# A windowed attention stack on one core: the mask written by ScalarE, the norms read back in one transfer, a fourth front buffer, and a new order of all engines

## The chip, the core and the metric

The kernel runs on one core of one Trainium2 chip. The metric is the device time of the whole program in microseconds (us), lower is better; every run is one execution of the same program. The core has five engines that work side by side and wait for each other through semaphores: TensorE (PE in the rows, PEld for its weight loads), VectorE (DVE), ScalarE (ACT), GpSimd (POOL), and SyncE (SP), which here issues every DMA transfer. SPq in the rows is SP's queue issuing a transfer.

## What is computed

The program has two phases. The first is a dense causal attention layer with 16 heads over 4 batches of 512 tokens, width 128, with a residual. The change hardly touches it. The second is a stack of 6 layers, each of a local attention and a feed-forward block:

```python
q, k = l2norm(q) * qs, l2norm(k) * ksc          # norm over the 64 lanes of a head
q = q*cos*scale + rotate_half(q)*sin*scale      # k alike, with 1/scale
sim = einsum('bhwie,bhwje->bhwij', bq, bk2)*8   # 32 queries x 64 keys: own window and the one before
attn = softmax(where(mask, -big, sim))          # band mask
x = x + (attn @ v) @ Wo ; then layer norm, W1, a*gelu(gate), W2
```

Everything is float32, but for the mask, which is kept as bfloat16 zeros and -1e25.

## The kernel before

**Tiles and steps.** The second phase is cut into 24 steps (6 layers by 4 batches), each step into 4 tiles of 128 tokens: 96 tiles `g`. For each tile there is one front `f`: fronts come in pairs for half a sequence (256 tokens), an even `f` makes the keys, an odd `f` the queries. Tile pair `2hu`, `2hu+1` needs fronts `2hu` and `2hu+1`.

**A front.** `pe_front` multiplies by the weights into PSUM in four parts; ACT squares each part (`act_square`, L785), DVE multiplies it by the two rotary tables (`dve_products`, L799 and L800, into `T1` and `T2`), POOL adds the turned half (`pool_rotate`, L805). `pe_square_sums` (L813) adds the squares of each head. Then the inverse root is made: `dve_clamp`, `act_guess` (Ln, L826, and Exp, L828) and three DVE steps of `dve_newton`, the last at L837, into `RN`. The inverse norms go out to a small DRAM tensor `norms` (`sp_norms_out`, L843) and come back spread over all 128 partitions into `RB` (`sp_norms_in`, L850, four transfers of 32 partitions). `pool_scale` (L857) multiplies `T1` by `RB`. `sp_relayout` moves `T1` to the places of keys (`KZ`, 8 transfers, L876) or queries (`QP`, 4 transfers, L870). `RB` is one buffer: the load for `f` waits until `pool_scale(f-1)` is done.

**A tile.** `pe_scores` (L906 to L918) fills a PSUM bank for each half of the heads: four bf16 matmuls of `identb` by `band` (L912) write the mask, 16 matmuls add the scores. DVE takes the maximum and subtracts it, ACT takes the exponential, DVE sums, POOL normalises (L955), PE turns the probabilities (`pe_turn_probs`, L965), ACT keeps them, and `pe_values` (L990) multiplies by `U`, which `pe_u` (L891) makes in four parts, each kept by ACT (L898).

**The feed-forward block** of each step is spread over later tiles: turn (L1083), six up products one after another through PSUM bank 6 (L1109), gelu on ACT (L1115, which loads its table), gate on DVE, down (L1131). `next_vo` (L1010) makes the weights of a later step.

**The order** is written out by hand: `pe_slot(k)`, `act_slot(k)`, `dve_slot(k)`, `pool_slot(k)` and `sp_slot(k)` list what each engine does for slot `k`, one slot per tile. An engine takes its list strictly in order, so a wait holds everything behind it. The lines that set the order of SP:

```python
def sp_slot(k):
    if hold_f(k + 4): sp_norms_in(k + 4)
    ...
    if hold_f(k + 5): sp_norms_out(k + 5)
    if hold_f(k + 4): sp_relayout(k + 4)
```

Of the kernel before, what the change touches and what calls it, by code (L numbers as in the profile page):

```python
# [52 lines left out]
def build(nc, x, wq, wk, wv, wr, w1, w2, b2, rot, qsc, wqk, wvt, wos, lngt, lnbt, b1t, out):  # L53
    pe, act, dve, pool, sp = nc.tensor, nc.scalar, nc.vector, nc.gpsimd, nc.sync
    with ExitStack() as keep:
# [4 lines left out]
        XM = sb('XM', [P, TILES, E])  # L60
# [74 lines left out]
        with ExitStack() as ctx:  # L135
# [233 lines left out]
            def act_early_keep(b):  # L369
                r = slice(b * TPB, (b + 1) * TPB)  # L370
                act.wait_ge(s_res, PAIRS * (b + 1))
                act.activation(XM[:, r, :], X[:, r, :], ACT.Copy).then_inc(s_exm, 1)

            def act_dense_program():
                act_ln_keep(0)
                for h in range(-3, 2 * UNITS + 3):
# [19 lines left out]
                    if side == 0 and PAIRS <= u < UNITS and u % PAIRS == 4:  # L396
                        act_early_keep(u // PAIRS - 1)
# [68 lines left out]
            def dve_early_scale(b, t):  # L466
                dve.wait_ge(s_erstd, b + 1)
                dve.wait_ge(s_exm, b + 1)
# [128 lines left out]

            def sp_dense_program():
# [8 lines left out]
                for q in range(HG):  # L607
                    sp.wait_ge(s_vod, q)
                    in_dma(sp, s_vo0, WVS[:, :], wvt[q])
                    in_dma(sp, s_vo0, WOS[:, :], wos[q])  # L610

# [17 lines left out]
        with ExitStack() as ctx:  # L629
# [5 lines left out]
            T1 = [sbl(f'T1{i}', [P, HG, 2, HALF]) for i in range(3)]  # L635
# [21 lines left out]
            norms = [nc.dram_tensor(f'norms{i}', (P, HALF), F32).ap() for i in range(2)]  # L657
# [28 lines left out]
            l_scores_done = sig('scl', 2, 'pe', 5)  # L686
            l_max_done = sig('nml', 2, 'dve')
# [29 lines left out]
            lxm = sig('lxm', 1, 'act')  # L717
# [69 lines left out]
            def dve_products(f, i):  # L787
# [3 lines left out]
                if i == 0:  # L791
                    dve.wait_ge(l_folded.sem, l_folded.at(s // BATCH * 4 + 2 * hf + kind))
                    if f >= 3 and kind:
                        dve.wait_ge(s_kz, 128 * ((f - 3) // 2 + 1))
                    elif f >= 3:
                        dve.wait_ge(s_qp, 64 * ((f - 3) // 2 + 1))
                dve.wait_ge(l_squared.sem, l_squared.at(f, i))
                dve.wait_ge(l_rotated.sem, l_rotated.at(f, i - 2))
                dve.tensor_tensor(T1[f % 3][:, i, :, :], v, TAB[:, kind, 0, :, cols], ALU.mult)  # L799
                dve.tensor_tensor(T2[i % 2][:, :, :], v, TAB[:, kind, 1, :, cols], ALU.mult).then_inc(l_products.sem, 1)  # L800

            def pool_rotate(f, i):
                pool.wait_ge(l_products.sem, l_products.at(f, i))
                t1 = T1[f % 3][:, i, :, :]
# [34 lines left out]
            def sp_norms_out(f):  # L839
                sp.wait_ge(l_newton.sem, l_newton.at(f))  # L840
                if f >= 2:
                    sp.wait_ge(s_rb, 64 * (f - 1))
# [406 lines left out]
            def act_slot(k):  # L1249
                if here(k):  # L1250
                    act_exp(*tile(k), 1)
# [305 lines left out]
```

## Time and profile before

| what | value |
|---|---|
| median of 3 runs | 2100.08 us (2099.58 to 2102.47) |
| the profiled execution: own time / span of the core | 2099.16 us / 2097.3 us |
| granted TensorE clock, mean | 0.989 |
| busy share of PE, DVE, ACT, POOL | 97%, 72%, 63%, 69% |
| first phase, filling, steady tiles, tail | to about 511, to 560, to about 2072, to 2097.3 us |

The profiled execution took 1.9 us more than its span, outside the span. Matmuls are pipelined and their ends are modelled, so PE's busy share says less than the distance from the start of one group of matmuls to the start of the next.

### The profile page before, as it was taken

What the parts mean: (1) busy time and instruction counts of PE and PEld (TensorE: products, weight loads), DVE (VectorE), ACT (ScalarE), POOL (GpSimd) and SP (SyncE); (2) the same over time, 40 slices, a digit from 0 to 9 for tenths busy, and PEclk for the clock granted to TensorE, in tenths of its full rate; (3) what the DMA queues carried; (4) which work ended last, traced back from release to release, by engine and by line L of the source; (5) the groups of instructions that cost most, each with busy time, mean ns of one, the idle gap of its engine ahead of it and who ended that gap; (6) DMA issues with size and microseconds to landing.
All of it is one profiled execution on the core that took longest, in us unless ns stands there. A gap on an engine that the chain in (4) does not pass through costs nothing.

```text
span 2097.3 us, 61286 instructions
## 1 busy us (share of the span) xinstructions
PE 2029.8 (97%) x23760; PEld 1292.7 (62%) x23760; DVE 1501.0 (72%) x3291; ACT 1330.2 (63%) x2522; POOL 1453.3 (69%) x1439
## 2 busy tenths in 40 slices
PE   8999999998689999999999999999999999999997
PEld 4555555554456666666666666666666666666654
DVE  5666666665677777777877777877777877777853
ACT  5666666665356567666667676667666667666654
POOL 3344443433678888878877888878977888878852
PEclk9999999999799999999999999999999999999999
DMA  4000000000444554455454464454644455444441
GB/s 134 6 1 6 1 1 6 1 1 6 109 108 123 144 151 110 123 129 159 124 127 110 127 175 117 119 126 126 172 120 107 122 139 160 121 121 118 120 109 28
DMA packets 218416, 204.96 MB, mean 98 GB/s; under 512 B 32403, under 2 KB 211601, under 8 KB 218129
## 3 DMA queue, kind: packets, MB, share of 16 engines
q1 hardware_dynamic: 218128, 201.04, 37.1%
q8 instruction: 191, 3.13, 0.6%
q14 instruction: 97, 0.79, 0.1%
HBM read 83.53 MB, written 13.63 MB: 46 GB/s over the span
## 4 chain that ended last, share of the span: by engine, by line
SPq 25%; POOL 20%; DMA 14%; PE 12%; issue 3%; ACT 0%; DVE 0%; DVEq 0%; ACTq 0%; POOLq 0%
POOL T L857 20%; DMA RB<-norms 14%; SPq L876 10%; SPq L850 8%; SPq L870 7%; PE bank L891 3%; PE bank L779 3%; PE bank L1109 1%; PE bank L918 1%; PE bank L990 1%; PE bank L965 1%; PE bank L1131 1%; PE bank L813 1%; PE bank L912 0%; PE bank L1010 0%
## 5 line engine op out<-in xcount | busy, mean ns | idle before, releaser
L857 POOL TENSOR_TENSOR T<-T,RB 128x512 f32<-128x512 f32 x384 | 480.4, 1285 | 213.8 <-DMA RB<-norms 213.8
L805 POOL TENSOR_TENSOR T<-T 128x512 f32<-128x512 f32 x384 | 491.7, 1283 | 78.4 <-DVE T L800 78.0
L891 PE MATMUL bank<-WU,XT 128*32 128x512 f32 x3072 | 414.3, 599 | 2.0 <-ACT U L898 1.9
L779 PE MATMUL bank<-XT,WQK 128*128 128x256 f32 x1536 | 401.0, 394 | 14.7 <-DVE T L800 13.1
L539 POOL TENSOR_SCALAR PR<-PR,RI 128x512 f32<-128x512 f32 x256 | 174.1, 694 | 291.0 <-DVE RI L439 289.9
L785 ACT ACTIVATE SQ<-bank 128x512 f32<-128x512 f32 x384 | 224.9, 600 | 237.4 <-PE bank L779 236.9
L779 PEld LDWEIGHTS bank<-XT,WQK 128*128 128x128 f32 x1536 | 277.2, 192 | 136.3 <-issue 68.5
L799 DVE TENSOR_TENSOR T<-bank,TAB 128x512 f32<-128x512 f32 x384 | 261.8, 682 | 124.5 <-ACT SQ L785 67.6
L898 ACT ACTIVATE U<-bank 128x512 f32<-128x512 f32 x384 | 228.8, 596 | 96.4 <-PE bank L891 95.8
L363 ACT ACTIVATE PR<-PR,NM 128x512 f32<-128x512 f32 x256 | 183.5, 718 | 147.1 <-DVE NM L434 145.7
L800 DVE TENSOR_TENSOR T<-bank,TAB 128x512 f32<-128x512 f32 x384 | 261.2, 680 | 0.0
L434 DVE CUSTOM_DVE_ANT_0 PR<-bank,causal 128x512 f32<-128x512 f32 x256 | 170.3, 684 | 108.8 <-PE bank L247 108.8
L918 PEld LDWEIGHTS bank<-KZ,QP 128*32 128x32 f32 x6144 | 177.2, 111 | 67.6 <-issue 51.4
L955 POOL TENSOR_TENSOR PL<-PL,RIL 128x512 f32<-128x512 f32 x192 | 202.4, 1055 | 20.2 <-DVE RIL L948 19.9
L990 PEld LDWEIGHTS bank<-U,PTL 128*32 128x32 f32 x5952 | 171.7, 110 | 58.4 <-issue 58.4
L918 PE MATMUL bank<-KZ,QP 128*32 128x128 f32 x6144 | 204.5, 274 | 0.0
L925 DVE TENSOR_REDUCE NML<-bank 128x8 f32<-128x512 f32 x192 | 131.9, 687 | 99.5 <-PE bank L918 99.4
L990 PE MATMUL bank<-U,PTL 128*32 128x128 f32 x5952 | 185.3, 273 | 0.8 <-issue 0.8
L972 ACT ACTIVATE PTL<-bank 128x512 f32<-128x512 f32 x192 | 114.2, 595 | 65.4 <-PE bank L965 65.2
L254 PEld LDWEIGHTS bank<-ident,PR 128*128 128x128 f32 x1024 | 112.8, 141 | 65.6 <-POOL PR L539 40.3
L1109 PE MATMUL bank<-XNT,W1S 128*114 128x512 f32 (+1 forms) x288 | 151.0, 609 | 2.3 <-ACT GE L1115 1.0
L945 DVE TENSOR_REDUCE RSL<-PL 128x8 f32<-128x512 f32 x192 | 130.4, 679 | 15.6 <-ACT PL L939 15.6
(124 smaller groups left out, 3059.0 us busy)
## 6 DMA issues: line engine op xcount, KB each, us to landing
RB<-norms SPq DMA_DIRECT2D x384, 128.0 KB, 3.3
KZ<-T SPq DMA_DIRECT2D x384, 128.0 KB, 2.5
QP<-T SPq DMA_DIRECT2D x192, 256.0 KB, 4.7
TAB<-rotary_dram SPq DMA_DIRECT2D x24, 512.0 KB, 5.2
norms<-RN SPq DMA_DIRECT2D x96, 128.0 KB, 1.7
WQK<-wqk_halves_dram SPq DMA_DIRECT2D x12, 512.0 KB, 6.2
WVS<-wv_turned_dram SPq DMA_DIRECT2D x29, 128.0 KB, 3.4
WOS<-wo_lanes_dram SPq DMA_DIRECT2D x29, 128.0 KB, 3.5
```

The lines of the kernel that those rows point to most:

```text
L779: m = pe.matmul(b[:, ab * HALF:(ab + 1) * HALF], WQK[n % 3][:, i, ab, :], XT[s % 2][:, hf * HALF:(hf + 1) * HALF], start=True, stop=True)
L785: act.activation(SQ[i][:, :, :], bank[5 * (i % 2)][:, :].rearrange('p (a c) -> p a c', a=2), ACT.Square).then_inc(l_squared.sem, 1)
L799: dve.tensor_tensor(T1[f % 3][:, i, :, :], v, TAB[:, kind, 0, :, cols], ALU.mult)
L800: dve.tensor_tensor(T2[i % 2][:, :, :], v, TAB[:, kind, 1, :, cols], ALU.mult).then_inc(l_products.sem, 1)
L805: pool.tensor_tensor(t1, t1, T2[i % 2][:, ::-1, :], ALU.add).then_inc(l_rotated.sem, 1)
L857: pool.tensor_tensor(t1, t1, RB[:, i:i + 1, :].to_broadcast([P, 2, HALF]), ALU.mult).then_inc(l_scaled.sem, 1)
L876: sp.dma_start(kz[:, :, pp, :], T1[f % 3][r:r + WIN, :, ab, :]).then_inc(s_kz, 16)
L891: i = pe.matmul(bank[1][h * WIN:(h + 1) * WIN, :], XT[s % 2][:, c0:c0 + WIN], WU[:, lp * HG + h, :], start=True, stop=True)
L898: act.activation(U6[(4 * g + w) % 6][:, :], bank[1][:, :], ACT.Copy).then_inc(l_u_kept.sem, 1)
L918: m = pe.matmul(o[:, 2 * pl:2 * pl + 2, :, :], QP[t // 2][:, pr, q0:q0 + WIN], KZ[t // 2][:, pr, :, q0:q0 + GRP].rearrange('p h (k j) -> p ...
L955: pool.tensor_tensor(o, o, r, ALU.mult).then_inc(l_probs_normed.sem, 1)
L990: i = pe.matmul(bank[7][w * WIN:(w + 1) * WIN, 0:E], PTL[half][:, 2 * k + gg, w * WIN:(w + 1) * WIN], u[:, grp * E:(grp + 1) * E], start=f ...
```

## The change

1. **Mask.** `act_mask(s, t, half)` lets ACT copy `band` (bf16) into the PSUM bank; `pe_scores` waits for it and its four mask matmuls are gone. All later matmuls add to the bank.
2. **Norms.** `norms` is now 32 rows of 4 x 256 values, so that the four rows in use are each one piece of 4 KB; they come back in one transfer that reads each row 32 times.
3. **Buffers.** `T1` has four buffers instead of three. Room comes from `XM`, the copy of the residual, which moves to a DRAM tensor `resid`: SP stores it (three times in the first phase, once between the phases) and loads it at the end into the first `T1` buffer. Four copies by ACT go.
4. **Order.** All five slot functions are written anew; the loops begin at slot -7 instead of -8.

The diff, cut to its core:

```diff
-            T1 = [sbl(f'T1{i}', [P, HG, 2, HALF]) for i in range(3)]
+            T1 = [sbl(f'T1{i}', [P, HG, 2, HALF]) for i in range(4)]
...
-            norms = [nc.dram_tensor(f'norms{i}', (P, HALF), F32).ap() for i in range(2)]
+            norms = [nc.dram_tensor(f'norms{i}', (WIN, HG * HALF), F32).ap() for i in range(2)]
...
-                sp.dma_start(norms[f % 2], RN[:, :]).then_inc(s_rn, 16)
+                sp.dma_start(norms[f % 2].rearrange('h (g c) -> g h c', g=HG), RN[:, :]).then_inc(s_rn, 16)
...
-                rows = norms[f % 2].rearrange('(g h) (a c) -> h a g c', h=WIN, a=1)
-                for h in range(HG):
-                    sp.dma_start(RB[h * WIN:(h + 1) * WIN, :, :], rows[h].to_broadcast([WIN, HG, HALF])).then_inc(s_rb, 16)
+                rows = norms[f % 2][0:HG, :].rearrange('h (a q) -> h a q', a=1).to_broadcast([HG, WIN, HG * HALF])
+                sp.dma_start(RB[:, :, :].rearrange('p g c -> p (g c)'), rows).then_inc(s_rb, 16)
...
+            def act_mask(s, t, half):
+                g = s * TPB + t
+                act.wait_ge(l_shifted.sem, l_shifted.at(g - 1, half))
+                act.activation(bank[2 + half][:, :], band[:, 0 if t == 0 else 1, :], ACT.Copy).then_inc(l_masked.sem, 1)
+
...
-                pe.wait_ge(l_shifted.sem, l_shifted.at(g - 1, half))
-                for w in range(4):
-                    r = slice(w * WIN, (w + 1) * WIN)
-                    pe.matmul(sbk[r, :], identb[:, r], band[:, 0 if t == 0 else 1, :], start=True, stop=False, skip_group_check=True)
+                pe.wait_ge(l_masked.sem, l_masked.at(g, half))
```

What the new slots do to the order is seen in the built programs. First **PE**, from the scores of one tile on (`WU,XT` is a part of `U`, `KZ,QP` the scores, `SQ,IND` the sums of squares, `XT,WQK` parts of a front, `U,PTL` the values, `ident,PL` the turned probabilities). Before:

```order
L891 MATMUL bank<-WU,XT 32x512 x4
L912 MATMUL bank<-band,identb 32x512 x4
L918 MATMUL bank<-KZ,QP 32x2x2x32 x16
L813 MATMUL bank<-SQ,IND 32x256 x8
L891 MATMUL bank<-WU,XT 32x512 x4
L912 MATMUL bank<-band,identb 32x512 x4
L918 MATMUL bank<-KZ,QP 32x2x2x32 x16
L779 MATMUL bank<-XT,WQK 128x256 x4
L891 MATMUL bank<-WU,XT 32x512 x4
L990 MATMUL bank<-U,PTL 32x128 x32
L891 MATMUL bank<-WU,XT 32x512 x4
L779 MATMUL bank<-XT,WQK 128x256 x2
```

And now, from the last sums of squares of a tile on:

```order
L817 MATMUL bank<-SQ,IND 32x256 x8
L894 MATMUL bank<-WU,XT 32x512 x4
L923 MATMUL bank<-KZ,QP 32x2x2x32 x32
L894 MATMUL bank<-WU,XT 32x512 x4
L995 MATMUL bank<-U,PTL 32x128 x14
L783 MATMUL bank<-XT,WQK 128x256 x4
L1136 MATMUL bank<-W2S,GE 128x128 x6
L995 MATMUL bank<-U,PTL 32x128 x14
L894 MATMUL bank<-WU,XT 32x512 x4
L970 MATMUL bank<-ident,PL 128x128 x4
L783 MATMUL bank<-XT,WQK 128x256 x2
L1136 MATMUL bank<-W2S,GE 128x128 x6
```

The masks are gone, both halves of the scores stand together at the head of the tile, the probabilities of the same tile are turned later in the same slot, and the sums of squares of the front stand at its end.

Then **SP**, in the middle of a layer change (`norms<-RN` goes out, `RB<-norms` comes back, `KZ<-T` and `QP<-T` are the relayouts, `TAB` and `WQK` are tables and weights). Before:

```order
L843 DMA norms<-RN 128x256
L870 DMA QP<-T 64x4x256 x4
L850 DMA RB<-norms 32x4x256 x4
L113 DMA TAB<-rotary_dram 128x4x256
L843 DMA norms<-RN 128x256
L876 DMA KZ<-T 32x4x256 x8
L850 DMA RB<-norms 32x4x256 x4
```

And now:

```order
L847 DMA norms<-RN 4x32x256
L113 DMA TAB<-rotary_dram 128x4x256
L853 DMA RB<-norms 128x1x1024
L879 DMA KZ<-T 32x4x256 x8
L847 DMA norms<-RN 4x32x256
L113 DMA TAB<-rotary_dram 128x4x256
L853 DMA RB<-norms 128x1x1024
L873 DMA QP<-T 64x4x256 x4
```

The load of `RB` stood behind the relayout of the front before; now it stands ahead of it, directly behind the norms that it waits for, and is one transfer instead of four.

Last **ACT**, around the slot in which gelu and the guess meet (`ACT_TABLE_LOAD` loads a function table; `LG<-SM` is the Ln and `bank<-LG` the Exp of the guess). Before:

```order
L898 ACTIVATE U<-bank 128x512
L1115 ACTIVATE GE<-bank,B1T 114x512
L826 ACT_TABLE_LOAD
L826 ACTIVATE LG<-SM 128x256
L828 ACT_TABLE_LOAD
L828 ACTIVATE bank<-LG 128x256
L898 ACTIVATE U<-bank 128x512
L939 ACTIVATE PL<-PL 128x512
L785 ACTIVATE SQ<-bank 128x512 x2
L898 ACTIVATE U<-bank 128x512
L939 ACTIVATE PL<-PL 128x512
L1115 ACT_TABLE_LOAD
L1115 ACTIVATE GE<-bank,B1T 113x512
```

And now:

```order
L1120 ACTIVATE GE<-bank,B1T 114x512
L901 ACTIVATE U<-bank 128x512
L830 ACT_TABLE_LOAD
L830 ACTIVATE LG<-SM 128x256
L832 ACT_TABLE_LOAD
L832 ACTIVATE bank<-LG 128x256
L901 ACTIVATE U<-bank 128x512
L1120 ACT_TABLE_LOAD
L1120 ACTIVATE GE<-bank,B1T 113x512
L1122 ACT_TABLE_LOAD
L901 ACTIVATE U<-bank 128x512
L944 ACTIVATE PL<-PL 128x512
```

The two table loads of the guess were followed by a part of `U`, the exponential and squares, and only then by the third gelu; now the third gelu with two more loads comes directly behind that part of `U`, ahead of the next exponential. `bank<-band` is the new mask copy.

## Rows read from the trace of the kernel before

**Rows 1.** The page: busy time, and the chain that ended last
```profile
PE 2029.8 (97%) x23760; PEld 1292.7 (62%) x23760; DVE 1501.0 (72%) x3291; ACT 1330.2 (63%) x2522; POOL 1453.3 (69%) x1439
...
SPq 25%; POOL 20%; DMA 14%; PE 12%; issue 3%; ACT 0%; DVE 0%; DVEq 0%; ACTq 0%; POOLq 0%
```

**Rows 2.** Windows: each engine in the steady stretch, (x) instructions
```profile
700.00:1900.00 1200.00, 1194.13 (x16652) 802.57 (x16648) 926.31 (x1864) 798.73 (x1407) 992.12 (x896) 1.00 0.51 132
```

**Rows 3.** Windows: L918 alone, the same stretch (PE, PEld)
```profile
700.00:1900.00 1200.00, 160.68 (x4864) 139.21 (x4864) 1.00 0.51 132
```

**Rows 4.** Timeline of PE over most of a tile (start, length, what)
```profile
1112.45 1.02 PE L1109 MATMUL bank<-XNT,W1S 128*114 128x512 f32 x2
1113.31 1.03 PE L779 MATMUL bank<-XT,WQK 128*128 128x256 f32 x4
...
1114.70 1.06 PE L891 MATMUL bank<-WU,XT 128*32 128x512 f32 x8
1115.58 0.40 PE L912 MATMUL bank<-band,identb 128*32 128x512 bf16 x4
1115.80 1.06 PE L918 MATMUL bank<-KZ,QP 128*32 128x128 f32 x32
1116.67 1.05 PE L813 MATMUL bank<-SQ,IND 128*32 128x256 f32 x16
1117.54 1.04 PE L891 MATMUL bank<-WU,XT 128*32 128x512 f32 x8
1118.39 0.40 PE L912 MATMUL bank<-band,identb 128*32 128x512 bf16 x4
1118.61 1.06 PE L918 MATMUL bank<-KZ,QP 128*32 128x128 f32 x32
1119.60 1.99 PE L779 MATMUL bank<-XT,WQK 128*128 128x256 f32 x8
```

**Rows 5.** Chain of waits, 1100 to 1135 (start, length, what)
```profile
by line: POOL T L857 35.8%; DMA RB<-norms 28.5%; SPq L876 16.4%; SPq L850 11.9%; SPq L870 10.2%; issue 3.2%; SPq L847 0.1%
...
1101.46 5.02 POOL T L857 x4
...
1114.24 3.54 DMA RB<-norms
...
1117.85 4.99 POOL T L857 x4
...
1129.52 3.19 DMA RB<-norms
...
1132.78 2.53 POOL T L857 x2
```

**Rows 6.** Timeline of SP's issues in the same stretch
```profile
1106.50 6.07 SPq L876 DMA_DIRECT2D KZ<-T  x8
1112.67 2.01 SPq L850 DMA_DIRECT2D RB<-norms  x4
...
1122.85 3.71 SPq L870 DMA_DIRECT2D QP<-T  x4
1126.66 3.30 SPq L850 DMA_DIRECT2D RB<-norms  x4
```

**Rows 7.** The page: DMA issues (count, size of one, us to landing)
```profile
RB<-norms SPq DMA_DIRECT2D x384, 128.0 KB, 3.3
KZ<-T SPq DMA_DIRECT2D x384, 128.0 KB, 2.5
QP<-T SPq DMA_DIRECT2D x192, 256.0 KB, 4.7
...
norms<-RN SPq DMA_DIRECT2D x96, 128.0 KB, 1.7
```

**Rows 8.** Timeline of ACT where gelu and guess meet
```profile
1117.06 1.28 ACT L826 ACT_TABLE_LOAD   x1
1118.35 0.42 ACT L826 ACTIVATE LG<-SM 128x256 f32<-128x256 f32 x1
1118.79 1.28 ACT L828 ACT_TABLE_LOAD   x1
1120.08 0.39 ACT L828 ACTIVATE bank<-LG 128x256 f32<-128x256 f32 x1
1120.41 0.58 ACT L898 ACTIVATE U<-bank 128x512 f32<-128x512 f32 x1
```

**Rows 9.** Timeline of DVE: last step of that Newton, and of the next
```profile
1121.42 0.42 DVE L837 SCALAR_TENSOR_TENSOR RN<-Y,bank 128x256 f32<-128x256 f32 x1
...
1136.05 0.42 DVE L837 SCALAR_TENSOR_TENSOR RN<-Y,bank 128x256 f32<-128x256 f32 x1
```

**Rows 10.** Timeline of SP in the filling of the pipeline
```profile
536.77 5.99 SPq L876 DMA_DIRECT2D KZ<-T  x8
542.87 1.97 SPq L850 DMA_DIRECT2D RB<-norms  x4
```

**Rows 11.** Windows: a QP relayout, and a stretch with one narrow transfer
```profile
556.00:557.00 1.00, 1.00 (x4) 0.82 (x3) 1.00 (x4) 0.00 (x0) 1.00 (x2) 0.50 0.88 180
658.90:660.20 1.30, 1.30 (x8) 1.07 (x7) 1.27 (x3) 0.97 (x2) 1.30 (x2) 1.00 0.08 23
```

**Rows 12.** Groups of the page: busy, mean ns of one, idle before and releaser
```profile
L857 POOL TENSOR_TENSOR T<-T,RB 128x512 f32<-128x512 f32 x384 | 480.4, 1285 | 213.8 <-DMA RB<-norms 213.8
L805 POOL TENSOR_TENSOR T<-T 128x512 f32<-128x512 f32 x384 | 491.7, 1283 | 78.4 <-DVE T L800 78.0
...
L898 ACT ACTIVATE U<-bank 128x512 f32<-128x512 f32 x384 | 228.8, 596 | 96.4 <-PE bank L891 95.8
...
L955 POOL TENSOR_TENSOR PL<-PL,RIL 128x512 f32<-128x512 f32 x192 | 202.4, 1055 | 20.2 <-DVE RIL L948 19.9
...
L925 DVE TENSOR_REDUCE NML<-bank 128x8 f32<-128x512 f32 x192 | 131.9, 687 | 99.5 <-PE bank L918 99.4
```

**Rows 13.** Timeline of PE: next weights (L1010) and values (L990)
```profile
1103.15 1.16 PE L1010 MATMUL bank<-WOS,WVS 64*128 64x128 f32 x8
1104.24 2.00 PE L779 MATMUL bank<-XT,WQK 128*128 128x256 f32 x8
...
1123.26 1.93 PE L990 MATMUL bank<-U,PTL 128*32 128x128 f32 x64
1125.01 1.04 PE L891 MATMUL bank<-WU,XT 128*32 128x512 f32 x8
```

More of the change, by code:

```diff
@@ L1241, in pe_slot @@
                     pe_u(*tile(k - 1), 1)
+                    pe_turn_probs(*tile(k - 1), 0)
+                if step_at(k - 8, LAST - 1):
+                    pe_ffn_up((k - 8) // 4, 4)
+                if hold_f(k + 3):
+                    pe_front(k + 3, 2)
                 if step_at(k - 7, LAST - 1):
@@ L1259, in act_slot @@
                 if here(k):
-                    act_keep_probs(*tile(k), 0)
-                    act_keep_u(*tile(k), 1)
+                    act_keep_probs(*tile(k), 1)
                 if hold_f(k + 4):
                     act_square(k + 4, 3)
-                if here(k):
-                    act_keep_probs(*tile(k), 1)
-                if step_at(k + 2, LAST):
-                    act_boundary((k + 2) // 4)
+                if step_at(k - 6, LAST - 1):
+                    act_ffn_gelu((k - 6) // 4, 1)
@@ L1268, in act_slot @@
                 if here(k):
                     act_keep_u(*tile(k), 2)
-                if step_at(k - 6, LAST - 1):
-                    act_ffn_gelu((k - 6) // 4, 1)
-                if step_at(k - 5, LAST - 1):
-                    act_ffn_scale((k - 5) // 4)
+                if step_at(k - 1, LAST):
+                    act_boundary((k - 1) // 4)
+                if hold_f(k + 4):
+                    act_guess(k + 4)
+                if here(k):
+                    act_keep_u(*tile(k), 3)
@@ L1316, in dve_slot @@
+            def dve_slot(k):
                 if step_at(k - 9, LAST - 1):
                     dve_ffn_gate((k - 9) // 4, 1)
-                if here(k - 1):
-                    dve_max(*tile(k - 1), 0)
                 if step_at(k - 11, LAST - 2):
@@ L1322, in dve_slot @@
                 if hold_f(k + 2):
+                    dve_products(k + 2, 2)
                     dve_clamp(k + 2)
+                    dve_products(k + 2, 3)
+                    dve_newton(k + 2)
+                if here(k - 1):
+                    dve_max(*tile(k - 1), 0)
                 if half_at(k + 3):
@@ L1398, in pe_layers_program @@
             def pe_layers_program():
-                for k in range(-8, TOTAL + 3):
+                for k in range(-7, TOTAL + 3):
                     pe_slot(k)
@@ L1409, in act_layers_program @@
                 act.preload_act_table_set('natural_log_exp_and_others')
-                r = slice((BATCH - 1) * TPB, BATCH * TPB)
-                act.activation(XM[:, r, :], X[:, r, :], ACT.Copy).then_inc(lxm.sem, 1)
-                for k in range(-8, TOTAL + 3):
+                for k in range(-7, TOTAL + 3):
                     if k == 0:
@@ L1422, in dve_layers_program @@
             def dve_layers_program():
-                for k in range(-8, TOTAL + 4):
+                for k in range(-7, TOTAL + 4):
                     if k == 0:
@@ L1437, in pool_layers_program @@
                 pool.sem_inc(l_folded.sem, 4)
-                for k in range(-8, TOTAL + 3):
+                for k in range(-7, TOTAL + 3):
                     pool_slot(k)
@@ L1444, in sp_layers_program @@
             def sp_layers_program():
+                r = slice((BATCH - 1) * TPB, BATCH * TPB)
+                sp.dma_start(resid[:, r, :], X[:, r, :]).then_inc(s_xm, 16)
                 sp_next_vo(0)
-                for k in range(-8, TOTAL + 3):
+                for k in range(-7, TOTAL + 3):
                     sp_slot(k)
+                sp_resid_back()
                 sp_shift(LAST)
```

235 lines of the change are left out of this document (118 added, 117 removed).

## The prediction

> **What bounds the kernel now.** I read the page first. PE is busy 97% of the span, the others 63 to 72%, yet the chain that ended last runs mostly over SP's queue, POOL and DMA and only 12% over PE [rows 1]. Two things can thus be the bound, and each has to be measured in the steady stretch, 700 to 1900 us.
>
> A tile takes 64 score matmuls of L918; 4864 of them in 1200 us are 76 tiles, so a tile takes 15.79 us [rows 3], and the 96 tiles about 1515 us. POOL works 992.12 us there, 13.05 per tile, DVE 12.2, ACT 10.5 [rows 2]: none is full.
>
> PE: busy shares of modelled ends prove little, so I take distances between starts in the timeline [rows 4]. A part of U takes 0.88 or 0.85 us, a half of the scores 0.87 and 0.99, the sums of squares 0.87, two parts of a front 1.83 or less. Four lanes of 32 columns run side by side in the first three; a 512-column f32 product on full width (L1109) takes 0.86. So a column costs the same wherever I look, and nothing stands between the groups: PE is at its column rate, with only tenths of a microsecond lost where a group changes. It is a true bound, or within some tenths of a microsecond of one.
>
> The other candidate is a ring through SP. In the chain of waits, 1101 to 1133, every piece begins where the one before ends: POOL scales front f (5.0 us), SP issues the relayout of f (6.07 us for keys, 3.71 for queries), then the four loads of RB (2.01 or 3.30), the last lands 3.2 to 3.5 after its issue, POOL scales f+1 [rows 5, 6]. From 1101.46 to 1132.78 are two fronts, 15.66 us each. POOL's wait for RB before each front, 213.8 us in all, 2.2 per front, is this ring [rows 12]. So before, PE and the ring are both at their limit, and a gain needs both to give way.
>
> **What the change does, part by part.**
>
> *Masks.* The four mask matmuls take 0.22 and 0.22 us from start to start (1115.58 to 1115.80, 1118.39 to 1118.61) [rows 4]: 0.44 per tile, 96 tiles, 42 us off PE. ACT takes two copies of 128x512 more. No row copies from SBUF into a bank at that size: the nearest are L898 (596 ns, from a bank) and the Exp of the guess, which writes 256 columns of a bank in 0.39 us [rows 8, 12], so 0.6 each, at the most 0.78. ACT goes from 10.5 to 11.7 us per tile. This lies beside PE, since the copy for the next tile stands between the exponentials, a slot ahead. If that cover went, each copy would hold up the scores by its 0.6.
>
> *SP's ring.* RB for f+1 is now asked for ahead of the relayout of f, so the ring is scale, one issue (0.5), landing, scale. Even with a landing of 8 us it is 5.0+0.5+8 = 13.5: it no longer binds. Three issues of about 0.5 go from SP too. What binds in its place is a longer path: the relayout of f now stands behind norms out and RB in of f+1, hence behind the Newton steps of f+1. The path is: sums of squares of f+1, Newton, norms out, RB issue, relayout of f, scores. The order gives it one whole tile and a piece: from the end of the sums in one slot, over the next slot, past U (0.88) and an up product (0.86) or the next weights (1.1), and an up product behind the sums in the worst tile: some 18 us [rows 4, 13]. The terms: Newton ends 4.3 us after the sums in the tile where gelu takes the table away (1117.54 to 1121.84), else 2.9 (1133.55 to 1136.47), and one more tenth or three since a product stands in between [rows 4, 9]; norms out 1.7 [rows 7]; RB's issue 0.5; relayout of queries to the last landing 2.3 + 4.7 = 7.0, and 2 more because RB's 512 KB are ahead of it. That is 15.7 in the worst tile: 2 us to spare. Of the fourth buffer: products of f need the relayout of f-4 landed, not f-3; since the relayout is later by some 5 us now, this pays for the delay, and costs nothing itself.
>
> *The single transfer.* It is the unknown cost. Before, four transfers take 1.4 us of issue and 3.3 of landing, 4.7 to 5 together [rows 6, 7]. Lower bound: the 1.7 of norms out, for a quarter of the bytes. Upper bound: all goes over few engines. One row shows what a narrow transfer does: with 0.08 of 16 engines busy, one and a little more, 23 GB/s flow [rows 11]. Four engines would need 131 KB each at 22, 6.0 us; the ends are what norms out takes beside its 8 KB per engine, 1.7 - 0.4 = 1.3; together 7.3. I take 5 to 6 as its effect on POOL: RB is needed about 6 us after it is asked for, since four rotations of 1.28 and two normalisations of 1.05 (7.2 us) now stand between two scales [rows 12].
>
> *Order.* The turned probabilities are now due in the same slot as their scores. Between scores and turning PE has U, half the values, two front parts, half the values and U again: 0.87+0.9+1.8+0.9+0.88, 5.4 us and the second half's scores, 0.87: 6.2 us or more [rows 4, 13]. The chain beside it is maximum, shift, exponential, sum, reciprocal on DVE and ACT, each 0.6 to 0.7 (six of them), then POOL's 1.05: 4.7 to 5.5 us [rows 12]. It fits. The one place where it doesn't is the slot after the gelus. ACT makes the guess with two table loads (1117.06 to 1120.47) [rows 8], then keeps the last part of U and at once loads again, the third gelu, and loads again: 3.4 us of work ahead of the next exponential. PE waits there for U, for the up product that needs the bank, or for the probabilities; laid side by side I get 0.5 us, once per four tiles, 24 x 0.5 = 12 us.
>
> *Residual in DRAM.* Four copies of 0.6 go off ACT, which has room; the transfers are 256 KB, issued a batch before they are needed; the one between the phases is hidden by the fill, 50 us long. Nothing.
>
> *Fill.* The first load of RB after a relayout of keys starts 6 us after it could (536.77 to 542.87) [rows 10]; that comes forward. The relayout of queries on which the first scores wait goes back behind the next norms, by about as much. Nothing, plus or minus 5.
>
> **Sum.** 2099.2 - 42 + 12 = 2069 of its own time; the median of the runs shown lies 0.9 above the profiled one: 2070. As a tile: 15.79 - 0.44 + 0.13 = 15.48.
>
> **The rivals.**
>
> *The wide transfer turned narrow (slower), 0.28.* If RB comes over four engines, the relayout behind it queues on those four. They have 6.0 us of RB and then 64 KB of relayout each. A relayout of queries flows at 180 GB/s with 0.88 of the engines busy [rows 11], 11 to 13 GB/s for each: 5.3 us more, so that the last piece lands 0.8+6.0+5.3+0.5 = 12.6 us after RB's issue. Norms out, in four blocks now, would take 1.1 more. Then the path is 4.4+2.8+0.1+12.6 = 19.9 in the worst tile and 18.7 in the other that waits, against 18: 1.9 and 0.7 too late, 2.6 per four tiles, 0.65 per tile, 62 us, and 5 for the fill: 2137. If those four engines go at 22 GB/s once alone, the path just fits. It decides against the change from a mean delay of 0.3 us per tile on. For it speaks that RB's source has four rows as its outer step; against it, that the path has slack if the engine rate is the higher one. The Trainium skill (DMA: Bandwidth & Descriptors, "Why a DMA increments its semaphore by 16 and not by 1") says that the number of engines is the largest up to 16 that divides the slowest dimension of both sides: here 4. By that rule the narrow case is the one that happens, and only its price is open; the trace's narrow stretch agrees with it, but no run here shows it for RB. The same page, "Rules for kernel authors", advises one 128-partition transfer in place of several to part of the partitions, by which the single one would be no slower.
>
> *All waits vanish, 0.15.* The small losses at group changes that I read as PE's own are partly the ring's, and the guess costs nothing: 15.2 us per tile, -57 us, 2043; with half of it 2050.
>
> *Nothing gained, 0.10.* Another chain holds the old pace, most likely DVE to ACT to POOL for the probabilities, since they lost a slot of slack: 0.44 per tile eaten, 2097 to 2101.
>
> **How the numbers follow.** Likeliest, 0.47: PE bound, masks gone, small waits: 2070, its own range 2058 to 2088. The measurement tells about 0.2%, 4 us, from no change. Faster is the likeliest and the vanishing waits, 0.62; same is most of the third, 0.08; slower is the narrow case and the rest, 0.30. The range reaches down to 2050, which leaves out 0.05, and up to 2125, where the narrow case is half through, which leaves out some 0.13.
>
> **What the profile after would show.** PE: distances as before, no L912, a tile of 15.3 to 15.5 us. POOL's wait for RB below 0.5 us per front. SP's ring no longer in the chain, PE in its place. RB landing at 5 to 6 us; at 7 or more the narrow case is on, and the scores (L923) would wait for QP's landing, which they never do now. ACT between the third gelu and the next exponential: if PE stands there more than 1 us, the third term was too small. I am wrong altogether if a tile takes 15.8 us or more with PE waiting in one place of every slot.

## The result, and the profile after

The changed kernel takes 2360.66 us (median of 4 runs, 2353.85 to 2365.46) beside 2101.27 for the one before (4 runs, 2099.58 to 2103.76): ratio 1.1224, 95% interval [1.1196, 1.1253]. It is slower by 259 us, where 2070 was forecast and the range ended at 2125.

The page, busy time and chain, which answers to [rows 1]:

```profile
PE 2098.2 (89%) x22992; PEld 1315.0 (56%) x22992; DVE 1503.6 (64%) x3291; ACT 1433.8 (61%) x2708; POOL 1454.6 (62%) x1439
...
PE 54%; DMA 10%; issue 8%; POOL 4%; DVE 1%; SPq 1%; ACT 1%; DVEq 0%; ACTq 0%; POOLq 0%
```

SP's queue has left the chain, as forecast, and PE is in its place. But PE now stands idle, 8% of the chain is "issue", and PE's busy time went up by 68 us although 768 matmuls are gone. Windows over the steady stretch, all engines first, then L923 (the scores, L918 before) alone; they answer to [rows 2, 3], and the two last numbers but one are the granted clock and the DMA share:

```profile
700.00:1900.00 1200.00, 1064.19 (x13558) 698.44 (x13559) 785.93 (x1578) 750.08 (x1321) 837.66 (x755) 0.93 0.49 110
...
700.00:1900.00 1200.00, 170.37 (x4096) 153.09 (x4096) 0.93 0.49 110
```

4096 score matmuls are 64 tiles: 18.75 us a tile, against 15.79. The groups of the page, and its DMA issues, answer to [rows 12, 7]:

```profile
L860 POOL TENSOR_TENSOR T<-T,RB 128x512 f32<-128x512 f32 x384 | 479.6, 1279 | 400.5 <-DMA RB<-norms 400.5
...
L923 PE MATMUL bank<-KZ,QP 128*32 128x128 f32 x6144 | 253.1, 333 | 192.4 <-issue 192.4
...
RB<-norms SPq DMA_DIRECT2D x96, 512.0 KB
KZ<-T SPq DMA_DIRECT2D x384, 128.0 KB, 4.8
QP<-T SPq DMA_DIRECT2D x192, 256.0 KB, 6.8
```

POOL's wait for RB rose from 213.8 to 400.5 us, 4.2 per front. The relayouts land after 4.8 and 6.8 us instead of 2.5 and 4.7. And PE waits 192.4 us ahead of the scores, in 48 places, up to 8.3 us each. Before, it waited 0.0 us at the scores and 10.7 us, in 14 places, at the mask matmuls that stood ahead of them. The waits stand in every second tile, as `pe_scores` waits for the landing of `KZ` and `QP` only in the first tile of a pair. The name "issue" hides the releaser; SP, POOL and PE together show it. SP:

```profile
1221.48 0.58 SPq L847 DMA_DIRECT2D norms<-RN  x1
1224.79 0.57 SPq L853 DMA_DIRECT2D RB<-norms  x1
1225.44 3.73 SPq L873 DMA_DIRECT2D QP<-T  x4
1235.80 0.57 SPq L847 DMA_DIRECT2D norms<-RN  x1
1242.39 0.56 SPq L853 DMA_DIRECT2D RB<-norms  x1
```

POOL, then PE, the same stretch (in brackets the idle time before, and its releaser):

```profile
1228.36 2.50 POOL L809 TENSOR_TENSOR T<-T 128x512 f32<-128x512 f32 x2 [0.21 <-DVE T L804]
1237.38 4.93 POOL L860 TENSOR_TENSOR T<-T,RB 128x512 f32<-128x512 f32 x4 [6.52 <-DMA RB<-norms]
```

```profile
1215.81 1.05 PE L817 MATMUL bank<-SQ,IND 128*32 128x256 f32 x16
...
1218.71 1.93 PE L923 MATMUL bank<-KZ,QP 128*32 128x128 f32 x64
...
1234.63 0.38 PE L752 MATMUL bank<-ident,X 128*128 128x128 f32 x2
1240.78 3.64 PE L923 MATMUL bank<-KZ,QP 128*32 128x128 f32 x64 [5.76 <-issue]
```

RB is issued at 1224.79 and POOL can start only at 1237.38, 12.6 us later. The queries behind it are all issued by 1229.17, yet the scores that need them start at 1240.78. The DMA view of 1224 to 1242, in 40 slices of 0.45 us (tenths of the 16 DMA engines busy, and GB/s), says why:

```profile
DMA  2000207889899999999993122222222222221100
GB/s 84 0 0 0 18 9 196 203 212 228 191 168 178 180 155 168 105 100 127 198 137 50 36 73 91 80 82 75 82 80 82 87 84 86 86 66 48 43 20 0
```

Near 1233.5 the busy share falls from 0.9 to between 0.1 and 0.3, and from 1234.4 to 1239.8 some 80 GB/s flow. The window below has the share as 0.25, which is four engines of 16, near 20 GB/s each: they work off what is left. From 1239.8 on the traffic thins, and the scores start at 1240.78. What still flows then, up to 1241.5, is most likely the norms going out, issued at 1235.80, on which RB's load waits until 1242.39.

The wait costs twice. Windows around the same scores, the numbers after POOL's being the granted clock, DMA share and GB/s:

```profile
1236.00:1240.70 4.70, 0.00 (x0) 0.00 (x0) 0.00 (x0) 0.00 (x0) 3.32 (x3) 0.74 0.25 77
1240.80:1244.30 3.50, 3.50 (x68) 3.50 (x72) 1.53 (x3) 0.00 (x0) 3.50 (x4) 0.50 0.06 16
1245.30:1250.00 4.70, 4.70 (x84) 3.26 (x76) 3.52 (x7) 3.73 (x7) 2.08 (x2) 1.00 0.84 184
```

PE was idle, the granted clock fell, and the scores ran at 0.50, the 1.2 GHz level: 3.64 us for the 64 matmul records that take 1.93 in the tile without the wait (1218.71). At 1245.3 the clock is 1.00 again.

### The profile page after: what moved, and what is told of

Same layout as the page of the kernel before. It is cut to its first block, busy times and chain, and to the rows that moved or that the text cites. A ratio compares the mean times of both kernels' runs of the same rounds, so it can differ in the third digit from the quotient of the medians.

```text
span 2363.3 us, 59655 instructions
## 1 busy us (share of the span) xinstructions
PE 2098.2 (89%) x22992; PEld 1315.0 (56%) x22992; DVE 1503.6 (64%) x3291; ACT 1433.8 (61%) x2708; POOL 1454.6 (62%) x1439
## 4 chain that ended last, share of the span: by engine, by line
PE 54%; DMA 10%; issue 8%; POOL 4%; DVE 1%; SPq 1%; ACT 1%; DVEq 0%; ACTq 0%; POOLq 0%
PE bank L894 12%; PE bank L783 12%; PE bank L923 8%; DMA RB<-norms 6%; PE bank L995 6%; PE bank L1114 5%; PE bank L970 4%; POOL T L860 3%; PE bank L817 3%; PE bank L1136 2%; DMA norms<-RN 2%; DMA WQK<-wqk_halves_dram 1%; PE bank L1015 1%; POOL T L809 1%; SPq L879 1%
## 5 line engine op out<-in xcount | busy, mean ns | idle before, releaser
L860 POOL TENSOR_TENSOR T<-T,RB 128x512 f32<-128x512 f32 x384 | 479.6, 1279 | 400.5 <-DMA RB<-norms 400.5
L809 POOL TENSOR_TENSOR T<-T 128x512 f32<-128x512 f32 x384 | 481.7, 1276 | 35.7 <-DVE T L804 35.7
L894 PE MATMUL bank<-WU,XT 128*32 128x512 f32 x3072 | 437.5, 628 | 4.4 <-ACT U L901 2.2
L923 PE MATMUL bank<-KZ,QP 128*32 128x128 f32 x6144 | 253.1, 333 | 192.4 <-issue 192.4
L783 PE MATMUL bank<-XT,WQK 128*128 128x256 f32 x1536 | 391.4, 388 | 30.8 <-DVE T L804 22.0
L923 PEld LDWEIGHTS bank<-KZ,QP 128*32 128x32 f32 x6144 | 227.7, 135 | 230.8 <-issue 230.8
L995 PE MATMUL bank<-U,PTL 128*32 128x128 f32 x5952 | 208.3, 276 | 0.0
L970 PEld LDWEIGHTS bank<-ident,PL 128*128 128x128 f32 x768 | 85.3, 141 | 111.9 <-POOL PL L960 86.9
```

The lines of the kernel that those rows point to most:

```text
L783: m = pe.matmul(b[:, ab * HALF:(ab + 1) * HALF], WQK[n % 3][:, i, ab, :], XT[s % 2][:, hf * HALF:(hf + 1) * HALF], start=True, stop=True)
L809: pool.tensor_tensor(t1, t1, T2[i % 2][:, ::-1, :], ALU.add).then_inc(l_rotated.sem, 1)
L860: pool.tensor_tensor(t1, t1, RB[:, i:i + 1, :].to_broadcast([P, 2, HALF]), ALU.mult).then_inc(l_scaled.sem, 1)
L894: i = pe.matmul(bank[1][h * WIN:(h + 1) * WIN, :], XT[s % 2][:, c0:c0 + WIN], WU[:, lp * HG + h, :], start=True, stop=True)
L923: m = pe.matmul(o[:, 2 * pl:2 * pl + 2, :, :], QP[t // 2][:, pr, q0:q0 + WIN], KZ[t // 2][:, pr, :, q0:q0 + GRP].rearrange('p h (k j) -> p ...
L995: i = pe.matmul(bank[7][w * WIN:(w + 1) * WIN, 0:E], PTL[half][:, 2 * k + gg, w * WIN:(w + 1) * WIN], u[:, grp * E:(grp + 1) * E], start=f ...
```

## The experiments

Each ratio is against the kernel before, run on the same chip. The medians come from different chips, on which the kernel before took 2101.27 to 2105.34 us; a difference between two experiments on different chips is therefore uncertain by some 4 us.

**Norms wide both ways** (`a_wide_both`, called the wide version below). The changed kernel with the old layout of `norms`, so that `RB` comes in four transfers; masks, buffers and order stay.

```diff
-            norms = [nc.dram_tensor(f'norms{i}', (WIN, HG * HALF), F32).ap() for i in range(2)]
+            norms = [nc.dram_tensor(f'norms{i}', (P, HALF), F32).ap() for i in range(2)]
-                sp.dma_start(norms[f % 2].rearrange('h (g c) -> g h c', g=HG), RN[:, :]).then_inc(s_rn, 16)
+                sp.dma_start(norms[f % 2], RN[:, :]).then_inc(s_rn, 16)
-                rows = norms[f % 2][0:HG, :].rearrange('h (a q) -> h a q', a=1).to_broadcast([HG, WIN, HG * HALF])
-                sp.dma_start(RB[:, :, :].rearrange('p g c -> p (g c)'), rows).then_inc(s_rb, 16)
+                rows = norms[f % 2].rearrange('(g h) (a c) -> h a g c', h=WIN, a=1)
+                for h in range(HG):
+                    sp.dma_start(RB[h * WIN:(h + 1) * WIN, :, :], rows[h].to_broadcast([WIN, HG, HALF])).then_inc(s_rb, 16)
```

> The changed kernel with the old way of the norms alone: out in one transfer of 128 rows, back in four transfers of 32 partitions each; mask, fourth buffer and new order stay. Theory N (the transfers with four blocks as their outer step run over few engines, and hold up what is queued behind them): norms out lands in 1.7 us, the last of RB about 5 us after its first issue, PE's wait ahead of the scores goes, and the time is what was predicted for the change without this, about 2070, at most 2085. Theory O (the new order is at fault: relayout behind the next norms, probabilities due in the same tile): no more than 40 us come back from 2361, since the waits stay.

2066.86 us (2065.58 to 2067.35), ratio 0.9817 [0.9803, 0.9832]. Its page, busy time, chain, groups and issues:

```profile
PE 2009.1 (97%) x22992; PEld 1242.9 (60%) x22992; DVE 1495.7 (72%) x3291; ACT 1430.7 (69%) x2708; POOL 1457.1 (71%) x1439
...
PE 71%; issue 1%; DVE 1%; POOL 1%; ACT 0%; DMA 0%; SPq 0%; DVEq 0%; POOLq 0%; ACTq 0%
...
L861 POOL TENSOR_TENSOR T<-T,RB 128x512 f32<-128x512 f32 x384 | 481.8, 1288 | 19.9 <-DMA RB<-norms 19.7
...
L924 PE MATMUL bank<-KZ,QP 128*32 128x128 f32 x6144 | 186.4, 273 | 0.4 <-issue 0.4
...
RB<-norms SPq DMA_DIRECT2D x384, 128.0 KB, 3.2
KZ<-T SPq DMA_DIRECT2D x384, 128.0 KB, 2.9
QP<-T SPq DMA_DIRECT2D x192, 256.0 KB, 4.8
```

So the shape of two transfers costs 294 us, more than the whole loss of 259, and the rest of the change is a gain. Of the 299.8 us between the two spans (2363.3 and 2063.5), 192.0 are PE's idle time ahead of the scores and 89.1 its longer busy time; the other 18.7 are idle times elsewhere. The busy time grew by 66.7 us in the scores and by 23.2 in `U` behind them (L894, 437.5 us there, 414.3 here), and hardly in the rest.

**One transfer with 32 outer rows** (`b_one_wide`). As above, but `RB` in a single transfer whose outer step is the 32 repeats, not the four rows. It reads other rows of `norms` than the kernel should.

```diff
+                flat = norms[f % 2].rearrange('(h g) c -> h (g c)', g=HG)[0:HG, :]
+                rows = flat.rearrange('(a h) q -> a h q', a=1).to_broadcast([WIN, HG, HG * HALF])
+                sp.dma_start(RB[:, :, :].rearrange('p g c -> p (g c)'), rows).then_inc(s_rb, 16)
```

> One transfer for RB, as in the change, with pieces of 4 KB, but the repeating dimension (32) outermost in place of the four rows; norms out as one transfer of 128 rows. RB so gets rows in another order than the lanes need, and the norms lie in DRAM otherwise: the numbers computed are other ones, the work is the same. Theory N in its form 'the outer dimension of four is what hurts': as fast as the kernel with four transfers, 2060 to 2085. Rival 'one big transfer of 512 KB is slow as such': RB lands 10 us or more after its issue, and the time stays above 2250.

2066.95 us (2065.36 to 2070.41), 0.9821 [0.9805, 0.9837]; RB lands 5.0 us after its issue, and the relayouts behind it after 3.9 and 5.9 us, 1.0 and 1.1 later than in the wide version, without a cost in time. Being one transfer costs nothing and wins nothing; with the same bytes and the same four rows, the order of the two outer steps makes the difference.

**The two halves of the shape** (`c_in_narrow`, `d_out_narrow`). First only `RB` comes in narrow (four outer rows, 32 repeats inside; it too reads other rows), while the norms go out wide; then the other way round, out as in the changed kernel, in by four transfers.

```diff
+                rows = flat.rearrange('h (a q) -> h a q', a=1).to_broadcast([HG, WIN, HG * HALF])
```

> The changed kernel with norms out in one transfer of 128 rows again, and RB back as in the change, four rows outermost, each read 32 times (the rows are others than the lanes need; the work is the same). It parts the two narrow transfers. Theory N with RB as its main part: RB takes 11 to 12.5 us as in the changed kernel, and the time is 2280 to 2340. If the norms going out were the main part (5.4 to 6.5 us in many fronts, where 1.7 had been): below 2200.

```diff
+                for h in range(HG):
+                    row = norms[f % 2][h:h + 1, :].to_broadcast([WIN, HG * HALF])
+                    sp.dma_start(RB[h * WIN:(h + 1) * WIN, :, :].rearrange('p g c -> p (g c)'), row).then_inc(s_rb, 16)
```

> The changed kernel with norms out as in the change (four blocks outermost), and RB back in four transfers of 32 partitions with pieces of 4 KB. Theory N with RB as its main part: norms out takes about 3 us, since no narrow RB lies ahead of it, and the path of the relayout has room for 1 us more: 2065 to 2100. If norms out is slow by itself (5 us or more in each front): 2150 or more.

In narrow: 2271.57 us (2262.7 to 2279.29), 1.079 [1.0754, 1.0825]. Out narrow: 2072.4 (2069.29 to 2073.38), 0.9846 [0.983, 0.9863]. The load makes 205 of the 294 us, a little less than expected (2280 to 2340 had been forecast for it). The store alone makes 5.5, but 89 once the load is narrow too. The likely reason, which no run isolates, is that its 128 KB then queue on engines that still have RB and the relayout: from 1235.80 to 1242.39 above, norms out take 6.6 us; before they took 1.7 [rows 7].

**Eight outer rows** (`h_eight`). The load reads eight rows 16 times each (other rows again).

```diff
+                rows = flat.rearrange('h (a q) -> h a q', a=1).to_broadcast([8, 16, HG * HALF])
```

> One transfer for RB as in the change, but with eight rows outermost, each read 16 times (other rows than the lanes need: the numbers are other ones, the bytes and pieces are the same); norms out as one transfer of 128 rows. Theory N (the outer dimension sets over how many engines it goes): with four rows RB took 11 to 12.5 us, with 32 repeats outermost 5.0; with eight it lands after 6.5 to 7.5, and the time is 2067 to 2110. Rival (the distinct rows outermost, with a repeat inside, are slow as such): above 2200 as with four.

2152.97 us (2151.38 to 2164.93), 1.025 [1.0225, 1.0275]. That is between the cases of 32 and 4 outer rows, above what was expected. How many engines each load keeps busy can be read in the filling of the pipeline, where RB is alone in flight. The windows, in order, are of the kernels with 32, 8 and 4 outer rows, and the three last numbers are granted clock, DMA share and GB/s:

```profile
528.50:530.50 2.00, 1.31 (x19) 0.52 (x17) 1.26 (x2) 0.60 (x1) 0.70 (x1) 1.00 0.86 256
531.00:534.00 3.00, 1.44 (x18) 0.62 (x18) 1.94 (x5) 1.29 (x4) 0.00 (x0) 1.00 0.52 138
531.00:535.00 4.00, 1.59 (x19) 0.62 (x18) 2.90 (x7) 1.78 (x4) 0.35 (x1) 1.00 0.25 98
```

Shares of 0.86, 0.52 and 0.25 are some 14, 8 and 4 engines of 16. So the outer rows do set the number of engines. But eight engines move 17 GB/s each and four move 25, so that twice the engines carry only 1.4 times as much; this is part of why eight rows come out so near to four.

**RB alone** (`i_rb_alone`). The narrow load, with SP waiting until it has landed before it issues the relayout. This tells whether RB's 11 to 12.6 us are its own or come of company.

```diff
                 sp.wait_ge(l_scaled.sem, l_scaled.at(f))
+                sp.wait_ge(s_rb, 16 * min(f + 2, FRONTS))
```

> As c_in_narrow (only RB's load is narrow, its rows others than the lanes need), but SP waits until RB of the next front has landed before it issues the relayout behind it, so that RB has the DMA engines for itself. Theory S (what is issued behind RB shares its few engines and makes it late): RB lands 7.5 to 9 us after its issue, as the first load of the filling does (7.8), where c_in_narrow had 11 to 12.6; the time is no better than 2230, since the relayout now begins later. Theory Q (four engines reading four rows are as slow as 11 us by themselves once all else runs): RB still takes 10.5 or more.

2354.32 us (2346.33 to 2360.58), 1.1184 [1.1161, 1.1207]. SP's timeline, where each relayout is issued when RB has landed:

```profile
1201.81 0.59 SPq L854 DMA_DIRECT2D RB<-norms  x1
1209.60 5.24 SPq L881 DMA_DIRECT2D KZ<-T  x8
...
1222.66 0.60 SPq L854 DMA_DIRECT2D RB<-norms  x1
1230.67 3.77 SPq L875 DMA_DIRECT2D QP<-T  x4
```

RB alone takes 7.8 and 8.0 us, and between 1014 and 1461, 24 of 25 loads take 7.4 to 8.6. In the kernel where only the load is narrow, eight loads issued between 1087 and 1214 took 10.8 to 12.9, so some 3 to 5 us come from transfers issued behind it. Here POOL's wait for RB falls to 78.3 us and relayouts land in 2.6 and 4.3; but they are issued 8 us later, and the scores wait all the same, 171.8 us. The path has no room for RB's time in either order.

**Narrow transfers in the kernel before** (`g_before_narrow`). Its order keeps the relayout ahead of RB, with no relayout behind.

```diff
-                rows = norms[f % 2].rearrange('(g h) (a c) -> h a g c', h=WIN, a=1)
-                for h in range(HG):
-                    sp.dma_start(RB[h * WIN:(h + 1) * WIN, :, :], rows[h].to_broadcast([WIN, HG, HALF])).then_inc(s_rb, 16)
+                rows = norms[f % 2][0:HG, :].rearrange('h (a q) -> h a q', a=1).to_broadcast([HG, WIN, HG * HALF])
+                sp.dma_start(RB[:, :, :].rearrange('p g c -> p (g c)'), rows).then_inc(s_rb, 16)
```

> The kernel before with its own order, mask and three buffers, and only the norms' transfers of the change: out in four blocks, back in one transfer with four rows outermost. Theory N: RB lands 10 us or more after its issue here too, and since the relayout (4.9 us of issue on the mean) stands inside the ring, a tile takes 5.0 + 4.9 + 0.6 + 10 to 12, 20.5 to 22.5 us, 2550 to 2750 in all: worse than in the new order. Rival (the transfer hurts only because the new order puts the relayout behind it): 2100 to 2200.

2439.92 us (2435.7 to 2448.56), 1.1608 [1.1582, 1.1633]. The chain of waits:

```profile
1206.87 4.99 POOL T L856 x4
...
1215.70 9.70 DMA RB<-norms
...
1225.47 5.05 POOL T L856 x4
...
1235.86 10.09 DMA RB<-norms
```

This is the ring of [rows 5] with 9.7 and 10.1 us for RB, issue and landing together, where it had 5.2 and 6.5 (issue 2.01 and 3.30, landing 3.2 to 3.5): 18.6 us for the front shown, which has the short relayout, and 19.2 on the mean (4004 score matmuls in the 1200 us from 700 on). The expectation of 2550 to 2750 us was too high, since it took 0.6 and 10 to 12 for issue and landing. That the transfer hurts only with a relayout behind it is refuted; the new order even takes the narrow transfers 79 us better than the old one does.

**The masks, and the ring** (`e_mask_pe`, `f_before_mask`). On the wide version, masks back on PE; and, on the kernel before, masks by ACT and nothing else.

```diff
-                pe.wait_ge(l_masked.sem, l_masked.at(g, half))
+                pe.wait_ge(l_shifted.sem, l_shifted.at(g - 1, half))
+                for w in range(4):
+                    r = slice(w * WIN, (w + 1) * WIN)
+                    pe.matmul(sbk[r, :], identb[:, r], band[:, 0 if t == 0 else 1, :], start=True, stop=False, skip_group_check=True)
```

> The changed kernel with the old way of the norms (as in a_wide_both), and the mask written by PE again, four bf16 matmuls per half ahead of the scores; the copies on ACT go. Theory M (PE's column time is the bound once the ring through SP is gone, so the masks cost what they take there): 0.44 us per tile, 42 us more than a_wide_both's 2067, 2100 to 2112. Rival (the gain of a_wide_both comes from the order, and PE has slack): 2067 to 2080.

```diff
+                    act_mask(*tile(k + 1), 0)
+                    act_mask(*tile(k + 1), 1)
```

> The kernel before with its own order, norms and buffers, and only the mask moved to ACT: both copies for the next tile stand behind the second exponential. Theory R (before, the ring of scale, relayout, RB load through SP binds as much as PE): no gain, 2095 to 2105. Rival (PE alone was the bound): the masks' 42 us come off at once, 2058 to 2070.

Masks on PE: 2098.18 us (11 runs, 2095.96 to 2101.0), 0.9976 [0.9967, 0.9985]. Before with ACT's masks: 2109.03 (2107.18 to 2112.81), 1.0031 [1.0019, 1.0042]. In the first PE is the bound (72% of the chain that ended last), and the masks are 31 us of it, or 33 by the ratios; the expectation had 42. In the second the time even rises by 0.3%, clear of the noise and a little above the range expected. The chain is the old one, with POOL waiting for RB as before:

```profile
SPq 25%; POOL 19%; DMA 14%; PE 11%; issue 4%; ACT 2%; DVE 1%; ACTq 0%; DVEq 0%; POOLq 0%
...
L858 POOL TENSOR_TENSOR T<-T,RB 128x512 f32<-128x512 f32 x384 | 479.8, 1282 | 216.2 <-DMA RB<-norms 216.2
```

Each of the two bounds, taken away alone, moves the time by 0.3% at most; both together give 1.8%. The first of these runs takes away more than the ring, since it keeps the new orders and the fourth buffer.

**The relayout ahead of RB again** (`j_relayout_first`), on the wide version, with the other four orders as changed.

```diff
-                if hold_f(k + 5):
-                    sp_norms_in(k + 5)
                 if hold_f(k + 4):
                     sp_relayout(k + 4)
+                if hold_f(k + 5):
+                    sp_norms_in(k + 5)
```

> a_wide_both with one change: SP issues the relayout of a front ahead of RB's load for the next, as before the change. Theory R (the ring of scale, relayout issue, RB load is what bound the kernel before, beside PE): the ring is back at 5.0 + 4.9 + 0.6 to 1.5 + 4.7, 15.5 to 15.7 us per front, and 15 to 30 us are lost against 2067: 2082 to 2097. Rival (the order on SP does not matter, the fourth buffer and the other engines' order made the gain): 2063 to 2072.

2146.84 us (2141.9 to 2149.46), 1.0198 [1.0184, 1.0212]: the miss is upwards. The chain of waits shows the ring back, and a piece in it that the old order did not have:

```profile
1214.26 5.00 POOL T L861 x4
...
1227.09 3.88 DMA RB<-norms
...
1231.04 5.00 POOL T L861 x4
1236.04 2.47 POOL T L809 x2
1238.51 1.45 POOL PL L961 x2
```

Two rotations and the start of a normalisation stand behind POOL's scaling and are at times in the chain. From one scaling to the next are 16.8 us. So among the new orders, SP's alone is worth 80 us: with the old one put back among them, the kernel is 2% slower than the one before the change.

**Three front buffers** (`k_three`), on the wide version: `T1` with three, its waits moved to front f-3.

```diff
-            T1 = [sbl(f'T1{i}', [P, HG, 2, HALF]) for i in range(4)]
+            T1 = [sbl(f'T1{i}', [P, HG, 2, HALF]) for i in range(3)]
```

> a_wide_both with three front buffers instead of four: the products of a front wait for the landing of the relayout three fronts back. My reckoning put the fourth buffer's worth as the cover of the later relayout, some 5 us of slack. Theory B (it is needed): products wait for QP or KZ and 2 us or more per pair of tiles are lost, 2100 or more. Theory D (with wide transfers the relayout lands in time): 2064 to 2075.

2067.01 us (2066.05 to 2068.21), 0.9821 [0.9808, 0.9835]. The fourth buffer is worth nothing in the wide version; with narrow transfers it was not tried.

**Fewer changes of matmul shape on PE** (`l_grouped`, on the wide version): the second half of the values and part 1 of `U` directly behind the first half.

```diff
                     pe_values(*tile(k - 2), 0)
+                    pe_values(*tile(k - 2), 1)
+                if here(k - 1):
+                    pe_u(*tile(k - 1), 1)
...
-                    pe_values(*tile(k - 2), 1)
-                if here(k - 1):
-                    pe_u(*tile(k - 1), 1)
```

> a_wide_both with the second half of the values and the second part of U moved ahead of the front's first two parts on PE, so that products 32 columns wide stand together and one change there and back between widths falls away per tile. Theory W (each change of width costs PE 0.1 to 0.2 us, and PE is the bound): 0.2 to 0.35 us less per tile, 2035 to 2050. Rival (the front's parts then come too late for DVE and PE waits at the third part): no gain or a loss, 2065 to 2140.

2152.82 us (2150.85 to 2153.73), 1.0226 [1.0212, 1.024]. Its chain of waits, from the sums of squares on:

```profile
1211.12 0.91 PE bank L817 x16
...
1214.50 0.43 DVE RN L841
1214.95 1.72 DMA norms<-RN
...
1218.86 2.46 DMA KZ<-T
...
1222.02 0.69 DVE T L804
...
1222.76 1.13 PE bank L783 x4
```

The rival is right in kind and too mild: the front's parts came later, and the front's own path is now in the chain. PE waits 56.0 us for DVE's products (11.7 in the wide version), 27.2 for POOL's probabilities (2.5) and 25.1 for ACT's `U` (2.2). Its busy time falls by 3.9 us, from 2009.1 to 2005.2, where 0.2 us a tile would be 19; so nothing here speaks for a gain of that size, but ends are modelled, and whether grouping alone would win something is not told by this run.

## Why the prediction was wrong

**What bounds the kernel: held.** PE and the ring were both at their limit: with only one of them relieved the kernel takes 2098 or 2109 us, with both 2067.

**The single transfer: this step failed.** The prediction put it as "I take 5 to 6 as its effect on POOL", with 7.3 as the upper bound, and gave the relayout "2 more because RB's 512 KB are ahead of it". Alone RB takes 7.8 to 8.0, and in the changed kernel 11.2 (1204.88 to 1216.05) and 12.6. Even for a load by itself the bound was too low, and not for the rate: 104 GB/s flow between 1204.0 and 1208.5 in the run with RB alone, 26 per engine where 22 were taken, which is 5.0 us of the 7.8; the ends are the other 2.8, where 1.3 were taken. And the change puts the relayout right behind the load, on the same few engines. The text did see this for the relayout, not for RB itself.

What made the kernel slow is the path that the prediction gave 15.7 us, "2 us to spare": norms out took 3.3 us instead of 1.7, and from RB's issue to the scores are 16.0 us where 0.5 + 7.0 + 2 = 9.5 were forecast up to the last landing. POOL's wait for RB by itself is not the loss: with RB alone it fell to 78.3 us, and the time stayed at 2354. The prediction also read that the scores never wait for QP's landing in the kernel before. They do at times: of the 14 waits at the mask matmuls, which stand behind the same semaphores, the one at 590.57 ends 3.5 us after the last issue of a QP relayout (583.32 to 587.03).

**The narrow rival: right in kind, wrong in chance and price.** It was given 0.28 and 2137 us. Its path, in the slot that ends in the wait at 1240.78: from the end of the sums (1216.8) to norms out 4.7 (4.4 forecast), norms out 3.3 (2.8), from RB's issue to the scores 16.0 (12.6), in all 24.0 where the forecast had 19.9. The room was read rightly: PE was ready at 1235.02, 18.2 us after the sums (18). Instead of 1.9 it is 5.8 us late. Over the kernel the waits are 192 us, 8.0 per four tiles, where the rival had 2.6. The 3.4 us that RB and relayout take longer are one part of the price. The other is the clock, which no term held: PE idles and then runs the scores and some of `U` at half clock, 89 us in all. The Trainium skill (DMA: Bandwidth & Descriptors, "Why a DMA increments its semaphore by 16 and not by 1") takes the number of engines from the slowest dimension of both sides, 4, 8 or 16 here. By that rule the narrow case was certain; the DMA shares of 0.25, 0.52 and 0.86 agree with it, and so does the order of 2271.57, 2152.97 and 2066.95 us for 4, 8 and 32 outer rows. The chance should have followed it, and the narrow stretch of [rows 11], where a load of 56.5 KB into `W2S` is in flight: it was one row in its favour with none against.

**Masks: right in kind, 42 forecast, 31 to 33 measured.** The distances hold: in the version with masks on PE, each half's still take 0.22 us from start to start (timeline of PE):

```profile
1200.78 0.40 PE L921 MATMUL bank<-band,identb 128*32 128x512 bf16 x4
1201.00 1.06 PE L927 MATMUL bank<-KZ,QP 128*32 128x128 f32 x32
```

Some 0.1 us a tile is lost elsewhere. Between 1000 and 1300, in every fourth tile of the wide version (5 of 19), `U` starts 2.03 us after the scores and not 1.75 to 1.77, which makes 0.07 of it; why, and the rest, stays open.

**Order: 12 us forecast, not seen.** In the wide version PE's idle time ahead of `U`, the up products and the turned probabilities, the three places that the prediction named, is 4.4, 2.1 and 3.3 us over the whole program. The gelus don't hold it.

**The ring and the fourth buffer.** That the ring stops binding held with wide transfers: POOL's wait for RB is 19.9 us, 0.2 per front. The buffer costs nothing, as said; that it pays for the later relayout is not so in the wide version, as three do as well there.

**The likeliest case** forecast 2070 for transfers that stay wide, and that kernel takes 2067: -38 against the kernel before on its chip where the sum had -30. That the two lie so near is partly luck: the masks give 31 to 33 and not 42, the rest of the change wins 5 us (2103.40 to 2098.18, with the masks on PE) where the sum took 12 off, and the two errors have opposite signs. It is the best version here that computes what it should. The single transfer with 32 outer rows is as fast, but it reads other rows than the kernel needs; a single one that is wide and reads the right rows was not run.

## What to carry to other kernels

Before merging transfers, look at what the outermost step of each side counts: 32 repeats outside and four rows inside cost nothing here, four rows outside 205 us or more. The DMA share of a stretch in which the transfer is alone shows how many engines it has. Price a narrow transfer in company, for itself and for everything issued behind it, and add what PE loses in clock once it stands. Where two bounds lie side by side, test each with the other taken away, since alone neither shows its worth.

## What the runs showed of the hardware

- In the filling, with no relayout near, RB's 512 KB land after 4.1 us with 32 outer rows (527.16 to 531.23), 7.0 with 8 (528.64 to 535.61) and 7.8 with 4 (529.30 to 537.09). The loads keep some 14, 8 and 4 engines busy and move 256, 138 and 98 GB/s: 25 per engine with four, 17 with eight. Why the rate of one falls is open.
- A transfer issued later slows one issued earlier: 7.4 to 8.6 us for RB alone, 10.8 to 12.9 with a relayout behind it. In the filling of the changed kernel, where only the norms go out 4.9 us behind its issue, RB lands after 8.8 (529.07 to 537.90).
- The page gives no landing time for the loads with 4 or 8 outer rows, nor for the store in four blocks; it has to be read from the waits of the engine behind.
- After idle times of 3.2 and 5.8 us the next 64 matmuls took 3.31 and 3.64 us instead of 1.93, at a granted clock of 0.54 and 0.50. The length of the idle time alone does not tell it: where only the load is narrow, 2.70 us (at 1067.61) were followed by 1.96, and 1.97 us (at 1103.38) by 3.58.
